# A fused four-layer kernel: one core's queries' sums moved ahead, two output rows handed to ScalarE and GpSimd, and a second recurrence with merged scans

## The reference, cut to what matters

```
# layer 1 (x is 8 x 512 x 128; 16 heads of d = 8), first recurrence
q, k = l2norm(x @ Wq), l2norm(x @ Wk);  v = x @ Wv;  beta = sigmoid(x @ Wbeta)
for t:  state = state * (1 - beta_t * k_t k_t^T) + beta_t * v_t k_t^T      # elementwise, 8 x 8 a head
        out_t = state q_t
...
# layer 3 (16 heads, dk = 4, dv = 8), second recurrence
gk = log_sigmoid(h @ gk_w1 @ gk_w2 + gk_b2) / 16
for t:  S = exp(gk_t)[:, None] * S + k_t v_t^T;   out_t = q_t S
out = rms(out, rms_w) * silu(h @ Wg) @ Wo,  and an MLP behind it
```

## Time and profile before

| | |
|---|---|
| median of 3 runs | 919.09 us (919.08 to 920.31) |
| profiled execution, its own time | 920.64 us |
| profiled execution, its span | 918.9 us |
| PE busy | 780.5 us, 85% |
| DVE busy | 690.4 us, 75% |
| ACT busy | 629.1 us, 68% |
| POOL busy | 628.2 us, 68% |
| mean granted TensorE clock | 0.953 of full |

### The profile page before, as it was taken

One profiled execution on the slowest core, in us unless ns is written; L12 is line 12 of the kernel. 1 busy time (PEld: TensorE's weight loads), 2 busy tenths in 40 slices (PEclk: granted clock), 3 DMA queues, 4 the chain that ended last, 5 costly groups with the idle time before them and its releaser, 6 DMA issues.

```text
span 918.9 us, 18391 instructions
## 1 busy us (share of the span) xinstructions
PE 780.5 (85%) x6152; PEld 472.1 (51%) x6152; DVE 690.4 (75%) x2046; ACT 629.1 (68%) x970; POOL 628.2 (68%) x414
## 2 busy tenths in 40 slices
PE   4965765688998799278788989999999999999997
PEld 1443221224543357223234766777677777677775
DVE  7769799985786577598999878776766766666664
ACT  3855233313555586268778988898888888889895
POOL 4008899720677646467887997686868686868695
PEclk9977799879999799789999999999999999999999
DMA  5999400009100030342600000000000000000000
GB/s 150 118 119 185 138 0 0 18 6 242 41 18 8 21 85 25 115 117 56 194 1 1 1 2 2 12 0 12 0 12 0 12 0 0 12 0 12 0 13 14
DMA packets 52793, 40.48 MB, mean 44 GB/s; under 512 B 6059, under 2 KB 44734, under 8 KB 52734
## 3 DMA queue, kind: packets, MB, share of 16 engines
q1 hardware_dynamic: 49662, 37.28, 18.7%
q0 software_dynamic: 3072, 2.51, 1.0%
HBM read 18.07 MB, written 14.88 MB: 36 GB/s over the span
## 4 chain that ended last, share of the span: by engine, by line
PE 26%; POOL 24%; DVE 23%; issue 16%; ACT 8%; DMA 1%; DVEq 0%; POOLq 0%; SPq 0%; ACTq 0%
PE PS L1914 25%; POOL scratch L748 21%; DVE scratch L1378 3%; DVE PS L1369 2%; DVE resid L1577 2%; DVE scratch L1675 2%; DVE stats L1412 1%; PE PS L1921 1%; DVE scratch L1683 1%; POOL resid L734 1%; POOL disp L658 1%; ACT scratch L1202 1%; DVE scratch L1261 1%; ACT scratch L1198 1%; DVE resid L1425 1%
## 5 line engine op out<-in xcount | busy, mean ns | idle before, releaser
L748 POOL TENSOR_TENSOR scratch<-scratch 128x1024 f16<-128x1024 f32 x128 | 272.8, 2133 | 84.6 <-ACT scratch L1202 82.4
L1862 DVE SCALAR_TENSOR_TENSOR resid<-PS,coef,resid 128x128 f32<-128x128 f32 x512 | 144.1, 344 | 108.6 <-PE PS L1914 102.5
L1914 PEld LDWEIGHTS PS<-A,scratch 128*128 128x128 f16 x3456 | 203.4, 98 | 37.8 <-POOL scratch L748 4.8
L1914 PE MATMUL PS<-A,scratch 128*128 128x128 f16 x3456 | 217.1, 219 | 3.9 <-POOL scratch L748 1.6
L1914 PE MATMUL PS<-A 128*128 (+1 forms) x768 | 186.8, 379 | 0.7 <-DVE A L1706 0.2
L1198 ACT ACTIVATE scratch<-PS,cols 128x512 f32<-128x512 f32 x256 | 163.8, 683 | 25.8 <-PE PS L1914 16.7
L1202 ACT ACTIVATE scratch<-scratch 128x1024 f16<-128x1024 f32 x128 | 135.3, 1057 | 5.0
L1914 PE MATMUL PS<-scratch,ident 128*128 128x512 f32 x160 | 92.2, 701 | 46.1 <-DVE scratch L1378 45.5
L617 POOL TENSOR_TENSOR scratch<-A 128x1024 f32<-128x1024 f32 x32 | 76.0, 2395 | 69.3 <-DVE A L1349 56.1
L1914 PEld LDWEIGHTS PS<-A 128*128 128x128 f16 x768 | 70.7, 98 | 66.6 <-issue 0.7
L658 POOL DMA_INDIRECT disp<-A,scratch x64 | 62.9, 983 | 36.5 <-issue 30.2
(11 more groups left out here) (337 smaller groups left out, 1318.0 us busy)
## 6 DMA issues: line engine op xcount, KB each, us to landing
A<-A SPq DMA_DIRECT2D x22, 256.0 KB, 7.5
y_rows<-zeros SPq DMA_DIRECT2D x8, 512.0 KB, 6.0
A<-y_rows SPq DMA_DIRECT2D x14, 256.0 KB, 3.6
disp<-zeros SPq DMA_DIRECT2D x4, 528.0 KB, 21.7
resid<-in_L_attn_x SPq DMA_DIRECT2D x8, 256.0 KB, 3.9
A<-scratch SPq DMA_DIRECT2D x8, 256.0 KB, 7.3
A<-in_L_ffn_ew SPq DMA_DIRECT2D x1, 2048.0 KB, 12.2
A<-scratch SPq DMA_DIRECT2D x32, 64.0 KB, 2.0
```

The source lines that it names most:

```text
L748: pool.tensor_tensor(h_low[n % 4], h_full[n % 2], h_high[n % 4], SUB).then_inc(S("m1_low"), 1)
L1862: last = STT(out=resid[:, g, :], in0=bank(4 + e % 2)[:, t * C:(t + 1) * C], scalar=coef[b % 2][:, t, e:e + 1], in1=resid[:, g, :], op0=MUL ...
L1914: return nc.tensor.matmul(o, l, r, start=start, stop=stop)
```

## The change

In the first recurrence, PE sums all eight squares ahead of the first pair, instead of three, three and two behind the first three. Output rows 4 and 5 are no longer scaled by DVE out of PSUM: ACT copies them to SBUF between the two factors of the last pair of the next row, and POOL scales them in place behind its last addend of that row. The two finished rows are signalled by semaphores that had another use in the stage before, and SP, PE and the two engines wait for those.

In the second recurrence, the two scans of a pair become one over 1024 elements. For that the decay of each group's first token is made 0: the float16 parts of the gates are cleared there once, and the two steps that write them leave the token out. There are two state buffers, the second in `nr`, so that `scan(n)` waits for the product of pair n - 2. DVE's `gates` move from behind `read_out` of pairs 1, 5, 9 to ahead of `read_out` of pairs 2, 5, 9. The last group's gate projection on PE and its copy on ACT move behind the keys and sums, and behind the gates' exponential, of pair 2.

```diff
+        states1 = [pair(8), nr[:, 0:2, :]]          # was: state = pair(8)
+        BY_POOL = (4, 5)
+        def row_made(i):
+            if i in BY_POOL:
+                return S("sg_1_then_o_scaled"), at(B + BY_POOL.index(i))
+            return S("o_row"), at(i - sum(k < i for k in BY_POOL))
...  SP
             for d in range(D):
-                sp.wait_ge(S("o_row"), at(d))
+                sp.wait_ge(*row_made(d))
...  POOL, behind written(i, p)
+                    if i - 1 in BY_POOL and p == 3:
+                        pool.wait_ge(S("k_then_o_copied"), at(B + BY_POOL.index(i - 1)))
+                        pool.wait_ge(s_wo, 2)
+                        pool.tensor_tensor(vR[:, i - 1, :], vR[:, i - 1, :], nr[:, 1, :], MUL).then_inc(S("sg_1_then_o_scaled"), 1)
...  ACT, behind the factors of (i, j)
+                    if j == D - 2 and i - 1 in BY_POOL:
+                        act.wait_ge(S("r0_acc"), at(i * HALF - 1))
+                        A_(vR[:, i - 1, :], bank(6 + (i - 1) % 2), ACT.Copy).then_inc(S("k_then_o_copied"), 1)
...  ACT, second recurrence
-                A_(gate_hl[:, 0, c], whole_gate(m), ACT.Copy).then_inc(S("gate_high"), 1)
+                A_(gate_hl[:, 0, c][:, 1:T], whole_gate(m)[:, 1:T], ACT.Copy).then_inc(S("gate_high"), 1)
-                if n == 2:
-                    gk_copy(B - 1)
                 if n in (2, 6, 10):
                     gates_out(1 + n // 4)
+                if n == 2:
+                    gk_copy(B - 1)
...  DVE, first recurrence
                         dve.wait_ge(s_wo, 2)
-                        row_out(i - 1)
+                        if i - 1 not in BY_POOL:
+                            row_out(i - 1)
...  DVE, second recurrence
-                TT(gate_hl[:, 1, c], whole_gate(m), gate_hl[:, 0, c], SUB).then_inc(S("gate_low"), 1)
+                TT(gate_hl[:, 1, c][:, 1:T], whole_gate(m)[:, 1:T], gate_hl[:, 0, c][:, 1:T], SUB).then_inc(S("gate_low"), 1)
+            V.memset(gate_hl.rearrange("p s (m t) -> p s m t", t=T)[:, :, :, 0:1], 0.0)
             combine(0)
-                dve.wait_ge(S("r_prod"), at(n, 1))
-                for j in range(2):
-                    last = V.tensor_tensor_scan(out=state[:, j, :], data0=bank(2 + j), data1=cbuf[n % 2][:, j, :],
-                                                initial=0.0, op0=MUL, op1=ADD)
-                last.then_inc(S("r_scanned"), 1)
+                dve.wait_ge(S("r_prod"), at(n, 2))
+                V.tensor_tensor_scan(out=states1[n % 2].rearrange("p j t -> p (j t)"), data0=bank(2, 2).rearrange("p j t -> p (j t)"),
+                                     data1=cbuf[n % 2].rearrange("p j t -> p (j t)"), initial=0.0, op0=MUL,
+                                     op1=ADD).then_inc(S("r_scanned"), 1)
-                TT(prod[n % 2], bank(4, 2), state, MUL).then_inc(S("r_prod"), 1)
+                TT(prod[n % 2], bank(4, 2), states1[n % 2], MUL).then_inc(S("r_prod"), 1)
                     scan(n)
+                    if n in (2, 5, 9):
+                        gates(1 + n // 4)
                     if n in (3, 7, 11):
                         gates_low(1 + n // 4)
                     read_out(n)
-                    if n in (1, 5, 9):
-                        gates(1 + n // 4)
...  PE, first recurrence
+            pe.wait_ge(S("bk_ready"), at(HALF - 1))
+            square_sums(range(D))
                     if p == 0 and i >= 2:
-                        pe.wait_ge(S("o_row"), at(i - 2))
+                        if i - 2 in BY_POOL:
+                            pe.wait_ge(S("k_then_o_copied"), at(B + BY_POOL.index(i - 2)))
+                        else:
+                            pe.wait_ge(*row_made(i - 2))
                     last.then_inc(S("r0_acc"), 1)
-                    if n < 3:
-                        square_sums(range(3 * n, min(3 * n + 3, D)))
...  PE, second recurrence
                 if n == 2:
-                    project_gk(B - 1)
                     pe.wait_ge(S("v_copied7"), at(B - 1))
...
                 if n >= 2:
                     sum_up(n - 2)
+                if n == 2:
+                    project_gk(B - 1)
```

More of the change, by code:

```diff
@@ L126, in build @@
             "pool": ["kk_pool", "r0_c", "m1_low", "r_c", "r_pair", "ids5", "z_made", "x_b2", "w_low", "og1"],
-            "act": ["xT_copied", "k_copied", "sgm1", "sq_head", "beta_copied", "bk0_copied",
+            "act": ["xT_copied", "k_then_o_copied", "sgm1", "sq_head", "beta_copied", "bk0_copied",
                     "r0_decay", "r_coef", "p2_copied", "o_sq", "o_std", "x_std",  "hid5",
@@ L132, in build @@
                     "x_high"],
-            "dve": ["stats", "xn", "v_copied", "sg_1", "k_squared", "xT_low", "bk_ready", "kk_dve", "r0_scanned", "r0_prod", "o_row", "r_scanned", "r_prod",
+            "dve": ["stats", "xn", "v_copied", "sg_1_then_o_scaled", "k_squared", "xT_low", "bk_ready", "kk_dve", "r0_scanned", "r0_prod", "o_row", "r_scanned", "r_prod",
                     "yg5", "x_added", "xn7_first", "x_var",  "lg5_added", "picked", "placed", "slots", "eo", "moe_added",
@@ L252, in build @@
         cbuf = [pair(6), pair(7)]
-        state = pair(8)
+        states1 = [pair(8), nr[:, 0:2, :]]
         prod = [pair(9), pair(10)]
@@ L474, in _ @@
                 rows_b = slice(H * b, H * b + H)
-                sp.wait_ge(S("k_copied"), at(b))
+                sp.wait_ge(S("k_then_o_copied"), at(b))
                 sp.dma_start(kR[rows_b], kS[:, b, :]).then_inc(s_kin, 16)
@@ L484, in _ @@
                 sp.dma_start(vR[H * b:H * b + H], vS[:, b, :]).then_inc(s_vin, 16)
-            sp.wait_ge(S("k_copied"), at(B - 1))
+            sp.wait_ge(S("k_then_o_copied"), at(B - 1))
             for b in range(B):
@@ L788, in stage1 @@
                 act.wait_ge(S("proj_k"), at(b))
-                A_(A6[:, c], bank(3), ACT.Copy, scale=1.0 / SCALE).then_inc(S("k_copied"), 1)
+                A_(A6[:, c], bank(3), ACT.Copy, scale=1.0 / SCALE).then_inc(S("k_then_o_copied"), 1)
                 act.wait_ge(S("proj_b"), at(b))
@@ L792, in stage1 @@
                 act.wait_ge(S("proj_g"), at(b))
-                act.wait_ge(S("sg_1"), at(b, 2))
+                act.wait_ge(S("sg_1_then_o_scaled"), at(b, 2))
                 A_(sgm[u], bank(5), ACT.Sigmoid, scale=1.0 / SCALE).then_inc(S("sgm1"), 1)
@@ L1292, in stage1 @@
                 dve.wait_ge(S("sgm1"), at(b))
-                STT(out=sg0[:, c], in0=bank(5), scalar=1.0 / SCALE, in1=sgm[u], op0=MUL, op1=MUL).then_inc(S("sg_1"), 1)
+                STT(out=sg0[:, c], in0=bank(5), scalar=1.0 / SCALE, in1=sgm[u], op0=MUL, op1=MUL).then_inc(S("sg_1_then_o_scaled"), 1)
                 dve.wait_ge(S("proj_v"), at(b))
@@ L1948, in stage1 @@
                 pe.wait_ge(S("xT_low"), at(b))
-                for n, c, free, done in ((2, 0, "k_copied", "proj_q"), (3, 128, "k_copied", "proj_k"),
-                                         (6, 512, "sgm1", "proj_b"), (5, 256, "sg_1", "proj_g"),
+                for n, c, free, done in ((2, 0, "k_then_o_copied", "proj_q"), (3, 128, "k_then_o_copied", "proj_k"),
+                                         (6, 512, "sgm1", "proj_b"), (5, 256, "sg_1_then_o_scaled", "proj_g"),
                                          (4, 384, "v_copied", "proj_v")):
```

## The result

The changed kernel takes **907.06 us** (median of 4 runs, 906.68 to 908.12) against 919.7 us for the kernel before in the same session (919.08 to 926.44). The ratio is 0.9859, 95% interval 0.9834 to 0.9885: faster by 1.4%. The forecast was 905.3 us, range 902.3 to 910.0. In medians the change gained 12.0 us against the 919.09 that the forecast started from and 12.6 against 919.7, where 13.8 were forecast. The profiled execution took 906.78 us, and the sum of the prediction gave 906.8 for it. Its span is 905.0 us against 918.9; these are one execution of each kernel.

The account below looks back on a forecast made before the run. DVE was taken to be full in the first recurrence but for a 5.33 us hole, and no engine full in the second; 5.6 + 1.2 + 7.0 = 13.8 off 919.09 gave 905.3 us, range 902.3 to 910.0.

Parts of the forecast that it names:

- Squares first: First recurrence: square sums ahead of pair 0 remove DVE's wait for ACT's root; gain 5.6 us.
- Rows 4 and 5: First recurrence: DVE is spared two row scalings of 0.60 us, handed to ACT and POOL; gain 1.2 us.
- rival 4: First recurrence: POOL's slack gone, addends late; squares give 3.4, handed rows nothing; 908.7 us, chance 0.08.
- last sum at full clock: First recurrence: 0.6 us to the good, counted only in the low end, 902.8, of the forecast's own range.
- Second recurrence: Second recurrence, four terms summing to 8.0 us; 7.0 taken because of ACT and POOL, bounds 3.5 and 8.5.
- gates: Second recurrence: gates behind a scan instead of the product come as POOL is released; gain 3.9 us, bounds 2.2 and 4.8.
- one scan for two: Second recurrence: merged scan takes 2.28 us in place of 2.34; gain 1.0 us, bounds 0 and 1.0.
- two state buffers: Second recurrence: product to scan goes from 1.36 to 1.13 us on half the pairs; gain 1.8, bounds 0 and 3.7.
- PE at half clock: Second recurrence: shorter stalls spare half of DVE's 2.6 us of waits for PE; gain 1.3, bounds 0 and 2.6.
- Rival 1: First recurrence: square sums at half clock hold the first products up; 911.6 us, chance 0.07.
- Rival 2: Second recurrence: POOL and ACT set the pace, about 3.7 us; only the gates' stall goes; 908.8 us, chance 0.15.
- Rival 3: Second recurrence: PE falls to half clock for good; slower, 943 us if all 16 pairs do; chance 0.03.

Follow-up runs that it names:

- e1: Kernel before with only PE's eight square sums moved ahead of pair 0: 913.91 us against 920.51, ratio 0.9931.
- e2: Changed kernel with the square sums back behind the first three pairs: 912.42 us, ratio 0.9915.
- e8_before_again: Kernel before, unedited, run once more for a second profile on a slower chip: 939.36 us.
- e3: Changed kernel with all output rows scaled by DVE again: 908.38 us, ratio 0.9868.
- e12: Changed kernel with output rows 3 to 6 by ACT and POOL instead of 4 and 5: 906.32 us, ratio 0.9864.
- e13: Changed kernel with row 6 also by ACT and POOL and PE's head squares behind the next pair's decays: 931.35 us against 947.34, ratio 0.9836.
- e9_after_again: Changed kernel, unedited, run once more for a second profile on a slower chip: 931.15 us.
- e10: Changed kernel with two scans of 512 a pair in place of the merged one: 906.9 us against 919.02, ratio 0.9862.
- e4: Changed kernel with one state buffer, scan n waiting for product n - 1: 929.0 us against 942.7, ratio 0.9862.
- e7: Changed kernel with the whole second recurrence as before, except the cleared first tokens: 911.52 us, ratio 0.9914.
- e11: Changed kernel with PE's head squares one pair later, behind the next decays: 906.46 us, ratio 0.9855.
- e5: Changed kernel with the gates behind the products of pairs 2, 5 and 9: 936.77 us against 942.7, ratio 0.9938.

## Why the prediction came out right, point by point

**Squares first: right, with one input wrong.** Forecast 5.6, measured 5.64 (the inversion at 15.46 after scan 0 in place of 21.10) and 5.65 in `e1`. The step on the clock was wrong: the sums were put between 87 and 89.7, at 88.5, on the ground that the clock would be at half. It never fell, and they ended at about 87.1, the full-clock bound. The low clock at 81 to 82 followed PE's idle stretch of 10.02, and the edit took that stretch away: behind 2.57 us of idle time, and 2.82 in `e1`, the clock was still at 1.00. The wrong input made no difference, since ACT's order (the root behind factor 9, 91.64, forecast 91.1 to 91.6) set the time. `e2` gives 6.1 and `e8_before_again` an inversion 0.72 earlier than the first profile, so the hole itself varies by up to 1.2 us from one profile to another.

**Rows 4 and 5: right.** Forecast 1.2, measured 1.2 (`e3`). The slack in POOL that rival 4 doubted held for rows 4, 5 and 6, and was used up by row 3 (`e12`, `e13`). The last sum at full clock, which the prediction kept for the low end of its range, gave 0.55 more in the profile (the wait of `row_out(7)` for PE is 2.08), but `e9_after_again` is the same kernel and didn't have it. Of the 13.9 this 0.55 is luck.

**Second recurrence: the size right, the composition wrong.** Forecast 7.0, measured 7.19 in the two profiles. Term by term:

| term | forecast | measured | by |
|---|---|---|---|
| gates | 3.9 (2.2 to 4.8) | 3.5 | 6.61 us of gates became 3.09 |
| one scan for two | 1.0 (0 to 1.0) | 0.33 | `e10` |
| two state buffers | 1.8 (0 to 3.7) | 0.75 | `e4` |
| sum of these | 6.7 | 4.6 to 4.75 | 64.07 (`e7`) and 64.25 (`e8_before_again`) to 59.5 |
| PE at half clock | 1.3 (0 to 2.6) | 2.45 to 2.6, or 0 | 66.70 against 64.25 (`e8_before_again`), 64.07 (`e7`) |

The 3.5 is the difference of the gates' own lengths, not of a run with that edit alone at full clock; it fits, since 3.5, 0.33 and 0.75 add up to 4.6. The prediction's lower bound of 2.2 for the gates doesn't follow from its own limit of 1.86 a gate, which gives 1.0; it decides nothing here. The first three terms were 2.0 to 2.1 too large. The merged scan takes 2.29, not 2.28, and its gain of 0.05 a pair is partly taken by waits. The second buffer frees the scan of the product, but then it stands behind PE's decays, which PE starts at the end of the scan before. The prediction had named that and put half the pairs free. By `e11` and `e13`, which move PE's other work away from there, the decays and the gates' meetings with POOL were the next limits.

The fourth term was mis-sized the other way, and its mechanism fits the runs. In this recurrence half-clock steps stood only in profiles whose gates sat behind the products, and `e5`, which differs from the changed kernel in that alone, has six. The forecast spared half of the waits, and the profiles all of them but 0.8. But this term isn't a fixed sum: in two of the five profiles with the gates behind the products it was absent. The 7.19 is thus 4.6 us of work order and about 2.6 that an execution of the kernel before pays or doesn't.

The forecast also took 1.0 off its sum of 8.0, for ACT and POOL. No row shows that loss: ACT's hole closed, DVE's scans waited for POOL as before (0.58 us at 433.35, 0.69 at 440.19 before), and what stands behind scan 15 moved by the whole gain. In effect the 1.0 paid for terms that were too large. So the errors offset each other, and the closeness of 906.78 to 906.8 is in part luck. It shows in the medians: the profiled execution of the kernel before, from which the terms were read, held half-clock stretches worth 2.45 and 0.55 us that another execution doesn't have, and the gain read from it was taken off a median 1.55 us lower. The median came out 1.8 us above the forecast. The range doesn't rest on this luck: with 4.6 in place of 7.0 the sum gives 907.7. (The forecast's own low end of 902.8 should be 903.2 by the terms named with it.) What makes the clock fall in one execution and not in the next, with rows equal to a hundredth or two, stays open.

**Rivals.** Rival 1 (sums at half clock): not seen, the clock was 1.00. Rival 2 (POOL's or ACT's pace): the forecast's pace of 3.5 to 3.6 became the rule only in `e11` and `e13`, where most plain pairs take 3.55; in the changed kernel most take 3.66 (444.98 to 448.64) to 3.79 (453.61 to 457.40), and the one wait in these is for PE's decays, not for POOL. So the rival's pace was about right and its reason wrong. ACT's hole ahead of keys 13 is closed, as forecast. Rival 3 (PE at half clock for good): not seen. Rival 4 (POOL's slack gone): not with two rows; with four, one scan waited 0.56 us for an addend and two more rows gave 0.20 us, far from the whole of the rival.

**How the parts add.** Undoing the squares costs 5.7 us of span (910.7 against 905.0), the rows 1.6 and the second recurrence 4.1. Together 11.4; the 13.9 of the first comparison holds before's half-clock share, 2.45, besides. These are spans of single executions: the 1.6 holds 0.55 of the slower last sum in `e3`. In medians the three are 5.4, 1.3 and 4.5, together 11.1.

## What to carry to other kernels

A stall can cost twice, once by its own length and once more where the granted clock falls behind it, as it did here in three of five profiles. Look at the granted clock of the stretch, not only at the waits. Where DVE and POOL hold each other up, place DVE's instruction where POOL has just been released rather than where it has just begun a long one. When a gap of the old profile shows a low clock, ask whether the edit removes the idle time behind it, before pricing the new work at half speed. And profile both kernels twice before a gain of 2 us, or of half a microsecond, is given to a cause.

## What the runs showed of the hardware

The same program, with PE's rows equal within 0.02 us up to the fall, ran one stretch at a granted clock of 0.92 in one execution and at 1.00 in another, and was 2.45 us apart over it. The Trainium skill (TensorE: Matmul & The Clock Gate, The HAM clock gate) says that the number of matmuls at low clock differs between runs of one kernel at its start. These rows show a difference of that kind in the middle of a kernel, and no run here shows its cause.

When an instruction of DVE and one of POOL hold each other up, hundredths of a microsecond decide which of them pays. With POOL ahead by 0.02 us the gate took 1.81 in place of 0.67. With both starting at 493.99 the gate took 0.67 and POOL's addition 1.80 in place of 1.28; the first gate of the changed kernel, at 439.11 with POOL's addition in the same hundredth, went the same way (0.67 and 1.79).
